# An attention and mixture-of-experts layer on one core: stores of q moved ahead of K's transfers, and each tile's rows turned between the halves of the tile before

## The chip, the cores and the metric

The kernel runs on one core of a Trainium2 chip. Its engines are TensorE (PE in the profile, its weight loads PEld), VectorE (DVE), ScalarE (ACT), GpSimd (POOL) and SyncE (SP), which here only issues transfers. The metric is the device time of one launch in microseconds (us), lower is better.

## The reference, cut to what matters

```python
# x (16,112,256); ctx (16,375,192); 16 heads of 16; 8 experts, 256 -> 512 -> 256, top 2
q = (layernorm(x) @ Wq);  k = ctx @ Wk;  v = ctx @ Wv          # per head
x = x + tanh(g_xattn) * (softmax(q k^T * hd**-0.5) v) @ Wo
xf = layernorm(x).reshape(b * s, d)                            # 1792 rows
probs = softmax(xf @ router_w.T);  keep the top 2, divide by their sum
h = silu(xf @ gate_w[e] + gate_b[e]) * (xf @ up_w[e] + up_b[e])
y = sum over the two chosen e of probs[e] * (h @ down_w[e] + down_b[e])
x = x + tanh(g_ffn) * y
```

## The kernel before, in words

**Precision.** Nearly every factor is split into a high part and a rest (`kH`/`kL`, `xH`/`xL`, `GH`/`GL`, `DH`/`DL`, `hH`/`hL`). A product is three matmuls: high by high, high by rest, rest by high. ACT makes the high part, DVE then subtracts it from the source for the rest.

**Attention.** First q is made for all 16 batches in four groups of four; `store_q(g)` writes group g to the DRAM scratch `q_scr` in four transfers, from where the heads are read back in another layout. Then a software pipeline runs in steps (`step`, one batch enters per step). In step n the context of batch n+2 is loaded (`load_ctx`), q of batch n is read (`queries`, six transfers and one for the bias row), K of batch n goes from `kH` and `kL` into `KS` (`keys`, eight transfers and four, which wait for ACT's and DVE's parts), and the negated row maxima of batch n-1 go into `QS` (line 306). All these transfers are issued by SP, strictly in the order of the code. The groups 2 and 3 of q are stored in steps 2 and 3, and step 4 (`FIRST - 1`) begins with a wait for them (line 288). From step 4 on, one expert's gate and up weights are loaded (line 291, `wsq`) in two steps of three; ACT squares and sums them (line 479, slot 4 of a step), for a scale per expert. ACT also takes the exponentials (line 496) on which PE's transposed scores (line 633) wait.

**Experts.** The rows are sorted by expert into 21 tiles of 256 rows (at most one expert a tile); POOL gathers a tile's rows (`xt`) and adds its results back (`acc_scr`). A step s handles three tiles: tile s is turned (four transposes, line 1347) and split into `xH` (ACT, line 1276) and `xL` (DVE, line 1506), and two small DVE operations pick its row weights; tile s-1 gets its gate and up matmuls (line 1363, 48 of them in two halves, `q` = 0 and 1, with a bank pair each), ACT's `sg` (line 1286, four chunks, a half makes two), DVE's `hf` (line 1523), then `hH` (ACT, line 1293) and `hL` (DVE, line 1529); tile s-2 gets its down matmuls (line 1376, 24), and `ys` on DVE (line 1538) and twice on ACT (line 1301). ACT and DVE work strictly in the order of their code.

**Arriving weights.** The first 8 steps are written out, and in them tile t < 8 needs expert t at most. While they run, the weights of expert s+1 are split in step s: `high(n)` on ACT (line 1033) and `low(n)` on DVE (line 1045) for gate (n even) and up (n odd), `down_high` and `down_low` (lines 1038 and 1052) for the down weights. Three raw buffers (`WB`) hold gate and up weights, so SP's load n waits for `low(n-3)`. PE's gate and up matmuls of tile t wait for `xL` of tile t, for `low(2t+1)`, and, for each half, for that half's `hf` of tile t-1:

```python
                        pe.wait_ge(v_x, t + 1)
                        if isinstance(i, int) and t < E:
                            pe.wait_ge(e_l, 2 * (t + 1))
                        for q in range(FQ):
                            wait(pe, a_s, FC * (t - 1) + FB * (q + 1))
                            wait(pe, v_h, FC * (t - 1) + FB * (q + 1))
```

Steps 8 to 19 are a loop on the engines, and 20 to 22 are written out again. At a step's start each of PE, DVE and ACT reads the tile's expert number from memory into a register (line 1159).

## Time and profile before

| | |
|---|---|
| median of 3 runs | 592.64 us (591.18 to 600.44) |
| the profiled execution, its own time | 591.52 us |
| its span, first to last instruction | 589.8 us |
| busy share of the span: PE, DVE, ACT, POOL | 83%, 72%, 58%, 50% |
| attention, with the first normalisation | 0 to about 340 us |
| routing | about 340 to 369 us |
| experts' tiles; copy to the output | 369 to about 575 us; the rest |

The profiled execution took 591.52 us, of which its instructions span 589.8; the 1.7 us around them are the launch. A stage's time is read from when its instructions start and end in the time-ordered list, and what an engine waited for stands in brackets at the end of its row.

### The profile page before, as it was taken

The numbers are of one execution on the slowest core, as the hardware profiler recorded it, in microseconds if no ns is written. First come the engines' busy times: TensorE is split into PE (matmuls) and PEld (weight loads), VectorE is DVE, ScalarE is ACT, GpSimd is POOL, SyncE is SP. The second block draws the span as 40 slices with busy tenths as digits, with TensorE's granted clock in tenths as the row PEclk, the third lists the DMA queues.
The fourth block names the chain that finished last, engine by engine and source line by source line (L and its number), as shares of the span: only waits on it lengthen the run. The fifth ranks groups of instructions, "written<-read, shape, count | busy, mean of one in ns | idle before, by whom it ended". The sixth has DMA issues, their size and how long they took to land. (4 is left out here: it accounts for less than half of the span.)

```text
span 589.8 us, 15126 instructions
## 1 busy us (share of the span) xinstructions
PE 487.2 (83%) x4723; PEld 437.1 (74%) x4724; DVE 427.2 (72%) x902; ACT 340.1 (58%) x638; POOL 293.0 (50%) x252
## 2 busy tenths in 40 slices
PE   4888897999999999999989721697899999999930
PEld 3767886888888888888868621596799999999920
DVE  4865897899998989989997678678775555555520
ACT  5743565766677666767654590767575545545410
POOL 5182555454565544564544323606457565555440
PEclk9997999999999999999995855799899999999985
DMA  8764668664566456446323086846524443343234
GB/s 205 184 151 104 167 163 181 175 165 112 136 139 180 92 162 177 114 102 159 74 48 103 23 303 192 297 161 168 155 37 75 72 62 54 62 71 54 28 37 133
DMA packets 69022, 74.88 MB, mean 127 GB/s; under 512 B 28744, under 2 KB 57248, under 8 KB 68784
## 3 DMA queue, kind: packets, MB, share of 16 engines
q1 hardware_dynamic: 60912, 63.23, 40.4%
q0 software_dynamic: 8064, 11.06, 11.3%
q8 instruction: 27, 0.44, 0.3%
q14 instruction: 19, 0.16, 0.1%
HBM read 42.51 MB, written 14.98 MB: 97 GB/s over the span
## 5 line engine op out<-in xcount | busy, mean ns | idle before, releaser
L363 POOL TENSOR_TENSOR PL<-PT 125x448 f16<-125x448 f32 x96 | 100.6, 1051 | 135.7 <-ACT PT L496 135.7
L496 ACT ACTIVATE PT<-bank 125x448 f32<-125x448 f32 x192 | 103.9, 544 | 85.1 <-PE bank L633 84.3
L790 DVE TENSOR_REDUCE mx<-bank 112x1 f32<-112x375 f32 x256 | 130.8, 542 | 24.6 <-PE bank L615 22.8
L1244 POOL DMA_INDIRECT acc_scr<-ys,slot_row x42 | 69.1, 1645 | 84.0 <-ACT ys L1301 75.1
L615 PE MATMUL bank<-KS,QS 97*112 97x376 f32 x256 | 91.5, 377 | 12.9 <-DVE mx L790 11.7
L633 PE MATMUL bank<-QS,KS 98*125 98x256 f32 x384 | 84.3, 304 | 4.7 <-ACT PT L496 3.1
L1363 PE MATMUL bank<-xH,GH 128*128 128x256 f16 x336 | 65.4, 277 | 7.7 <-ACT sg L1286 5.9
L633 PEld LDWEIGHTS bank<-QS,KS 98*125 98x125 f32 x384 | 67.0, 194 | 6.3 <-ACT PT L496 3.8
L1363 PE MATMUL bank<-xH,GL 128*128 128x256 f16 x336 | 65.3, 277 | 0.0
L1363 PE MATMUL bank<-xL,GH 128*128 128x256 f16 x336 | 65.2, 277 | 0.0
L615 PEld LDWEIGHTS bank<-KS,QS 97*112 97x112 f32 x256 | 45.5, 182 | 26.0 <-DVE mx L790 23.5
L780 DVE TENSOR_TENSOR PL<-PT 125x448 f16<-125x448 f32 x96 | 57.8, 618 | 6.5 <-ACT PT L496 6.4
L1058 POOL DMA_INDIRECT xt<-xn_scr,slot_row x42 | 45.8, 1091 | 30.8 <-DVE slot_row L1476 18.3
L652 PE MATMUL bank<-VS,PT 125*128 125x49 bf16 x768 | 52.1, 188 | 2.8 <-DVE PL L780 2.1
L1286 ACT ACTIVATE sg<-bank,gb,inv 128x256 f32<-128x256 f32 x84 | 42.5, 560 | 19.6 <-PE bank L1363 18.2
L1523 DVE SCALAR_TENSOR_TENSOR hf<-bank,ub,sg 128x256 f32<-128x256 f32 x84 | 37.5, 480 | 19.1 <-ACT sg L1286 18.2
L652 PE MATMUL bank<-VS,PL 125*128 125x49 bf16 x768 | 50.5, 185 | 0.0
L652 PEld LDWEIGHTS bank<-VS,PT 125*128 125x128 bf16 x768 | 39.4, 100 | 13.3 <-DVE PL L780 2.4
L1363 PEld LDWEIGHTS bank<-xH,GH 128*128 x336 | 33.3, 99 | 13.4 <-issue 9.1
L1301 ACT ACTIVATE ys<-ys,slot_weight 128x256 f32<-128x256 f32 x42 | 19.0, 500 | 41.9 <-DVE ys L1538 41.9
L1529 DVE TENSOR_TENSOR hL<-hf,hH 128x1024 fp32r<-128x1024 f32 x21 | 25.8, 1227 | 23.6 <-ACT hH L1293 23.6
L652 PEld LDWEIGHTS bank<-VS,PL 125*128 125x128 f16 x768 | 38.2, 97 | 0.0
(215 smaller groups left out, 1076.0 us busy)
## 6 DMA issues: line engine op xcount, KB each, us to landing
KS<-kH SPq DMA_DIRECT2D x128, 94.0 KB, 2.2
KS<-kL SPq DMA_DIRECT2D x64, 94.0 KB, 2.2
QS<-q_scr SPq DMA_DIRECT2D x96, 56.0 KB
ctx_sb<-in_ctx SPq DMA_DIRECT2D x16, 281.2 KB
wsq<-in_L_ffn_gate_w SPq DMA_DIRECT2D x8, 512.0 KB, 3.7
wsq<-in_L_ffn_up_w SPq DMA_DIRECT2D x8, 512.0 KB, 4.9
w_raw<-in_L_ffn_gate_w SPq DMA_DIRECT2D x8, 512.0 KB, 6.1
w_raw<-in_L_ffn_up_w SPq DMA_DIRECT2D x8, 512.0 KB, 4.3
```

The lines of the kernel that those rows point to most:

```text
L363: pool.tensor_tensor(PL[:, 2 * k:2 * k + 2, :, 0:N], PT[:, 2 * k:2 * k + 2, :, 0:N], PH[:, 2 * k:2 * k + 2, :, 0:N], ALU.subtract).then_in ...
L496: act.activation(PT[:, 2 * k:2 * k + 2, :, 0:N].rearrange("p a e i -> p (a e) i"), psST[k % 2][0:JP].rearrange("p (a i) -> p a i", i=NI)[: ...
L615: pe.matmul(psS[hd % 2][0:N, 0:MP], QS[u][0:RM, hd // 2, hd % 2, 0:N], KS[u][0:RM, hd // 2, :], start=True, stop=True).then_inc(p_S, 1)
L633: mm = pe.matmul(psST[k % 2][0:JP, 2 * NI * a:2 * NI * (a + 1)], KS[u][0:RM + 1, p, JP * t:JP * (t + 1)], QS[u][0:RM + 1, p, :, :].rearran ...
L652: mm = pe.matmul(psO[hd // 8][:, VW * (hd % 8):VW * (hd % 8 + 1)], P[:, JT * p + t, e, :], VS[:, u, t, hd, :], start=(part == 0 and t == 0 ...
L780: dve.tensor_tensor(PL[:, 2 * k:2 * k + 2, :, 0:N].rearrange("p a e i -> p (a e) i"), PT[:, 2 * k:2 * k + 2, :, 0:N].rearrange("p a e i -> ...
L790: dve.tensor_reduce(mx[:, hd:hd + 1], psS[hd % 2][0:N, 0:M], AX.X, ALU.max).then_inc(v_max, 1)
L1058: pool.indirect_dma_start(xt[:, t % XR, k, :], None, xn_scr, bass.IndirectOffsetOnAxis(ap=slot[:, TH * t + k:TH * t + k + 1].bitcast(U32), ...
L1244: pool.indirect_dma_start(acc_scr, bass.IndirectOffsetOnAxis(ap=slot[:, TH * t + k:TH * t + k + 1].bitcast(U32), axis=0), ys[:, u, k, :], ...
L1286: act.activation(sg[:, f, :], bG[f // FB][:, TS * (f % FB):TS * (f % FB + 1)], ACT.Silu, bias=gb[:, bass.ds(e * FC + f, 1)], scale=inv[:, ...
L1363: mm = pe.matmul(bank[:, TS * (f % FB):TS * (f % FB + 1)], w.rearrange("p o f -> p (o f)"), x[:, u, k, :], start=(n == 0 and k == 0), stop ...
L1523: dve.scalar_tensor_tensor(out=hf[:, f, :], in0=bU[f // FB][:, TS * (f % FB):TS * (f % FB + 1)], scalar=ub[:, bass.ds(e1 * FC + f, 1)], in ...
```

## The change

It has two parts.

1. In steps 2 and 3 of the attention, `store_q` of groups 2 and 3 (batches 8 to 15) is issued after the step's `queries` and before its `keys`, where it was issued at the step's end.
2. In the experts' steps the turning of tile s, with its `xH` and `xL`, moves from ahead of the matmuls of tile s-1 to between their halves (new functions `turn`, `rows_high`, `rows_low`); on ACT and DVE it stands after the first two chunks. The weight splits move too: `high(2s+2)` follows `xH`, `down_high` follows the fourth chunk, `high(2s+3)` goes behind `hH`; on DVE `low(2s+1)`, which belonged to the step before, now follows `xL` of tile s, `down_low` follows the fourth chunk and `low(2s+2)` stands behind `hL`. Step 0 has no tile in its halves: there the rows stand as before, then `high(2)`, `down_high(1)` and `high(3)`, and on DVE `down_low(1)` and `low(2)`. No operation is added or removed.

```diff
@@ -299,14 +299,14 @@
                     if live(i, c, 0):
                         if not starts(i, c):
                             queries(i, c)
+                            if isinstance(i, int) and 1 < NB * i + c < GROUPS:
+                                store_q(NB * i + c)
                             keys(i, c)
                     if live(i, c, 1):
                         b, h, u = at(i, c - 1)
                         sp.wait_ge(v_nm, b + 1)
                         sp.dma_start(f32(QS[u][RM:RM + 1, :, :, 0:N]).rearrange("o q e i -> o (q e) i"),
                                      f32(nm[:])).then_inc(d_m[u], 16)
-                    if isinstance(i, int) and 1 < NB * i + c < GROUPS:
-                        store_q(NB * i + c)
...
@@ -1150,6 +1150,10 @@
             return isinstance(i, int) and UN * i + c + 1 < E
+        def arrived(i, c):
+
+            return isinstance(i, int) and 0 < UN * i + c < E
...
@@ -1264,20 +1268,20 @@
...
+                def rows_high(i, c):
+                    t, h, u = at(i, c)
+                    act.wait_ge(k_T, t + 1)
+                    wait(act, k_GU, FQ * (t - 1))
+                    act.activation(xH[:, u], bT[u][:, 0:DC * TS].rearrange("p (c s) -> p c s", c=DC), ACT.Copy,
+                                   scale=XS).then_inc(a_x, 1)
+
                 def step(i, c):
...
-                    if has(i, c, 0):
-                        t, h, u = at(i, c)
-                        act.wait_ge(k_T, t + 1)
-                        wait(act, k_GU, FQ * (t - 1))
...
-                    if arriving(i, c):
-                        high(act, 2 * (UN * i + c + 1))
-                        high(act, 2 * (UN * i + c + 1) + 1)
+                    if has(i, c, 0) and not has(i, c, 1):
+                        rows_high(i, c)
                     if has(i, c, 1):
                         t, h, u = at(i, c - 1)
                         for f in range(FC):
@@ -1286,13 +1290,21 @@
...
                                            ).then_inc(a_s, 1)
-                            if f == FB - 1 and arriving(i, c):
-                                down_high(act, UN * i + c + 1)
+                            if f == FB - 1:
+                                if has(i, c, 0):
+                                    rows_high(i, c)
+                                if arriving(i, c):
+                                    high(act, 2 * (UN * i + c + 1))
+                        if arriving(i, c):
+                            down_high(act, UN * i + c + 1)
                         act.wait_ge(v_h, FC * (t + 1))
                         wait(act, k_D, t - 1)
                         act.activation(hH[:, u], hf[:], ACT.Copy).then_inc(a_h, 1)
                     elif arriving(i, c):
+                        high(act, 2 * (UN * i + c + 1))
                         down_high(act, UN * i + c + 1)
+                    if arriving(i, c):
+                        high(act, 2 * (UN * i + c + 1) + 1)
                     if has(i, c, 2):
...
@@ -1333,20 +1345,23 @@
...
+                def turn(i, c):
+                    t, h, u = at(i, c)
+                    x4, h4 = c % XR, i + c // XR
+                    pe.wait_ge(l_x[x4], 16 * TH * (h4 + 1))
+                    wait(pe, v_x, t - 1)
+                    for s in range(TH):
+                        for k in range(DC):
+                            mm = pe.transpose(bT[u][:, TS * k + 128 * s:TS * k + 128 * (s + 1)],
+                                              xt[:, x4, s, 128 * k:128 * (k + 1)], ident[:])
+                    mm.then_inc(k_T, 1)
+
                 def step(i, c):
                     if isinstance(i, int) and UN * i + c == 1:
                         pe.wait_ge(e_te, 1)
                     e1, e2 = two_experts(pe, i, c, kept)
-                    if has(i, c, 0):
-                        t, h, u = at(i, c)
...
-                        mm.then_inc(k_T, 1)
+                    if has(i, c, 0) and not has(i, c, 1):
+                        turn(i, c)
                     if has(i, c, 1):
                         t, h, u = at(i, c - 1)
                         pe.wait_ge(v_x, t + 1)
@@ -1364,6 +1379,8 @@
...
                             mm.then_inc(k_GU, 1)
+                            if q == 0 and has(i, c, 0):
+                                turn(i, c)
                     if has(i, c, 2):
...
@@ -1495,26 +1512,26 @@
...
+                def rows_low(i, c):
+                    t, h, u = at(i, c)
+                    x4, h4 = c % XR, i + c // XR
+                    dve.wait_ge(a_x, t + 1)
+                    dve.scalar_tensor_tensor(out=xL[:, u], in0=bT[u][:, 0:DC * TS].rearrange("p (c s) -> p c s", c=DC),
+                                             scalar=XS, in1=xH[:, u], op0=ALU.mult, op1=ALU.subtract
+                                             ).then_inc(v_x, 1)
+                    dve.wait_ge(l_x[x4], 16 * TH * (h4 + 1))
+                    wait(dve, a_y, TH * (t - UN + 1))
+                    dve.tensor_tensor(both_w[:, c % UN], xt[:, x4, :, DIM:ROWW],
+                                      which[:, bass.ds(TH * t, TH), :], ALU.mult).then_inc(v_b, 1)
+                    dve.wait_ge(v_b, t + 1)
+                    dve.tensor_reduce(wt[:, c % UN, :], both_w[:, c % UN], AX.X, ALU.add).then_inc(v_w, 1)
+
...
                 def step(i, c):
                     e1, e2 = two_experts(dve, i, c, kept)
-                    if has(i, c, 0):
-                        t, h, u = at(i, c)
...
-                        dve.tensor_reduce(wt[:, c % UN, :], both_w[:, c % UN], AX.X, ALU.add).then_inc(v_w, 1)
-                    if arriving(i, c):
-                        low(dve, 2 * (UN * i + c + 1))
-                        low(dve, 2 * (UN * i + c + 1) + 1)
+                    if has(i, c, 0) and not has(i, c, 1):
+                        rows_low(i, c)
                     if has(i, c, 1):
                         t, h, u = at(i, c - 1)
                         wait(dve, v_l, t)
@@ -1523,12 +1540,19 @@
...
                                                      op0=ALU.add, op1=ALU.mult).then_inc(v_h, 1)
-                            if f == FB - 1 and arriving(i, c):
-                                down_low(dve, UN * i + c + 1)
+                            if f == FB - 1:
+                                if has(i, c, 0):
+                                    rows_low(i, c)
+                                if arrived(i, c):
+                                    low(dve, 2 * (UN * i + c) + 1)
+                        if arriving(i, c):
+                            down_low(dve, UN * i + c + 1)
                         dve.wait_ge(a_h, t + 1)
                         dve.tensor_tensor(hL[:, u], hf[:], f32(hH[:, u]), ALU.subtract).then_inc(v_l, 1)
                     elif arriving(i, c):
                         down_low(dve, UN * i + c + 1)
+                    if arriving(i, c):
+                        low(dve, 2 * (UN * i + c + 1))
                     if has(i, c, 2):
```

In the blocks below, a row is an instruction or a run of equal ones in the engine's own order.

SP in the attention, from step 2's context load to step 4's first weight load, before (QS2, KS2 are batch 2's buffers, QS0, KS0 batch 3's):

```order
L260 DMA QS2<-q_scr 16x8x112 x6
L264 DMA KS2<-bias_scr 1x8x376
L278 DMA KS2<-kH 32x2x376 x8
L278 DMA KS2<-kL 32x2x376 x4
L306 DMA QS1<-nm 1x16x112
L329 DMA q_scr<-qP 128x4x112 x4
L252 DMA ctx_sb<-in_ctx_768 125x576
L260 DMA QS0<-q_scr 16x8x112 x6
```

and now:

```order
L260 DMA QS2<-q_scr 16x8x112 x6
L264 DMA KS2<-bias_scr 1x8x376
L329 DMA q_scr<-qP 128x4x112 x4
L278 DMA KS2<-kH 32x2x376 x8
L278 DMA KS2<-kL 32x2x376 x4
L308 DMA QS1<-nm 1x16x112
L252 DMA ctx_sb<-in_ctx_768 125x576
L260 DMA QS0<-q_scr 16x8x112 x6
```

The four stores moved ahead of K's twelve transfers; step 3 changes alike, so that the last thing ahead of step 4's wait is the transfer of `nm`.

DVE in step 2 of the experts (tile 2 turned, tile 1 in its halves), before:

```order
L1506 SCALAR_TENSOR_TENSOR xL<-bank,xH 128x512
L1511 TENSOR_TENSOR both_w<-xt,slot_choice 128x4
L1514 TENSOR_REDUCE slot_weight<-both_w 128x2
L1045 SCALAR_TENSOR_TENSOR GL<-w_raw,sc,GH 128x1024 x2
L1523 ISA
L1523 SCALAR_TENSOR_TENSOR hf<-bank,ub,sg 128x256
```

and now:

```order
L1540 SCALAR_TENSOR_TENSOR hf<-bank,ub,sg 128x256
L1519 SCALAR_TENSOR_TENSOR xL<-bank,xH 128x512
L1524 TENSOR_TENSOR both_w<-xt,slot_choice 128x4
L1527 TENSOR_REDUCE slot_weight<-both_w 128x2
L1045 SCALAR_TENSOR_TENSOR GL<-w_raw,sc,GH 128x1024
L1540 ISA
```

The first row now is the second chunk of `hf`: two chunks come ahead of `xL`, and one `GL` follows instead of two. The other stands at the step's end, between `hL` and the finished tile's `ys`:

```order
L1052 TENSOR_TENSOR DL<-DL,DH 128x1024
L1551 TENSOR_TENSOR hL<-hf,hH 128x1024
L1045 SCALAR_TENSOR_TENSOR GL<-w_raw,sc,GH 128x1024
L1562 ISA
L1562 SCALAR_TENSOR_TENSOR ys<-misc,inv,dbB 128x512
L1163 TENSOR_LOAD tile_e
```

The order on DVE is so: two chunks, rows, one rest, two chunks, `DL`, `hL`, one rest, `ys`; and ACT goes into the next step's `sg` right after its `ys`.

PE at the start of a step and in its first half, before:

```order
L1159 TENSOR_LOAD tile_e
L1159 ISA x2
L1347 MATMUL bank0<-ident,xt 128x128 x4
L1363 ISA
L1363 MATMUL bank2<-xH,GH 128x256
```

and now:

```order
L1163 TENSOR_LOAD tile_e
L1163 ISA x2
L1378 ISA
L1378 MATMUL bank2<-xH,GH 128x256
L1378 ISA
```

and, now, between the halves:

```order
L1378 MATMUL bank4<-xH,GL 128x256
L1355 MATMUL bank0<-ident,xt 128x128 x4
L1378 ISA
L1378 MATMUL bank3<-xH,GH 128x256
L1378 ISA
```

The transposes no longer stand between the read of the expert number and the first matmul that uses it.

## Rows read from the trace of the kernel before

**Rows 1.** Busy time by stretch, steps 4 and 5 of the attention: stretch, length, then each engine's busy us, granted clock, DMA share, GB/s.

```profile
82.10:102.80 20.70, 16.01 (x182) 14.16 (x183) 16.34 (x35) 12.12 (x22) 9.24 (x9) 1.00 0.76 180
102.80:120.70 17.90, 16.67 (x188) 14.93 (x188) 16.32 (x36) 12.74 (x25) 9.30 (x9) 1.00 0.68 173
```

**Rows 2.** SP in order of time, steps 2 to 4: start, length, then what it issued.

```profile
53.02 0.70 SPq L264 DMA_DIRECT2D KS<-bias_scr  x1
57.72 6.10 SPq L278 DMA_DIRECT2D KS<-kH  x8
...
74.49 5.18 SPq L278 DMA_DIRECT2D KS<-kH  x8
...
83.34 2.74 SPq L329 DMA_DIRECT2D q_scr<-qP  x4
88.73 0.38 SPq L291 DMA_DIRECT2D wsq<-in_L_ffn_gate_w  x1
```

**Rows 3.** ACT and PE in order of time, step 4 of the attention.

```profile
95.59 1.91 ACT L479 ACTIVATE wsq<-wsq 128x2048 f32<-128x2048 f32 x1 [2.93 <-DMA wsq<-in_L_ffn_up_w]
...
98.07 0.50 PE L633 MATMUL bank<-QS,KS 98*125 98x256 f32 x2 [2.48 <-ACT PT L496]
```

**Rows 4.** The chain that ended last: gate and up matmuls of tiles 2, 3, 7, 8.

```profile
391.33 5.44 PE bank L1363 x48
...
402.02 5.44 PE bank L1363 x48
...
442.82 5.24 PE bank L1363 x48
...
451.35 5.24 PE bank L1363 x48
```

**Rows 5.** Start of the tiles, in order of time, on DVE, PE and ACT.

```profile
370.78 0.69 DVE L1506 SCALAR_TENSOR_TENSOR xL<-bank,xH 128x512 f16<-128x512 f32 x1 [3.63 <-ACT xH L1276]
...
373.13 1.11 PE L1347 MATMUL bank<-ident,xt 128*128 128x128 f32 x4 [3.01 <-DMA xt<-xn_scr,slot_row]
...
376.60 0.40 PE L1363 MATMUL bank<-xH,GH 128*128 128x256 f16 x2
...
379.39 1.28 ACT L1286 ACT_TABLE_LOAD   x1
```

**Rows 6.** ACT in order of time, from the end of step 4 of the tiles.

```profile
406.74 0.91 ACT L1301 ACTIVATE ys<-ys,slot_weight 128x256 f32<-128x256 f32 x2 [1.95 <-DVE ys L1538]
407.55 0.57 ACT L1276 ACTIVATE xH<-bank 128x512 f16<-128x512 f32 x1
...
410.11 1.00 ACT L1286 ACTIVATE sg<-bank,gb,inv 128x256 f32<-128x256 f32 x2
```

**Rows 7.** DVE in order of time, step 5 of the tiles.

```profile
408.16 0.69 DVE L1506 SCALAR_TENSOR_TENSOR xL<-bank,xH 128x512 f16<-128x512 f32 x1 [1.46 <-ACT xH L1276]
...
409.20 2.48 DVE L1045 SCALAR_TENSOR_TENSOR GL<-w_raw,sc,GH 128x1024 f16<-128x1024 f32 x2
411.60 0.87 DVE L1523 SCALAR_TENSOR_TENSOR hf<-bank,ub,sg 128x256 f32<-128x256 f32 x2
412.39 1.22 DVE L1052 TENSOR_TENSOR DL<-DL,DH 128x1024 fp32r<-128x1024 f32 x1
...
415.51 1.23 DVE L1529 TENSOR_TENSOR hL<-hf,hH 128x1024 fp32r<-128x1024 f32 x1 [1.12 <-ACT hH L1293]
416.65 0.75 DVE L1538 SCALAR_TENSOR_TENSOR ys<-misc,inv,dbB 128x512 f32<-128x512 f32 x1
```

**Rows 8.** A weight load at the loop's turn; the last tile's first matmul; line 1159's register reads, min/median/max ns.

```profile
476.52 0.42 PEld L1347 LDWEIGHTS bank<-ident,xt 128*128 128x128 f32 x4 [0.26 <-issue]
...
553.50 0.39 PE L1363 MATMUL bank<-xH,GH 128*128 128x256 f16 x2
...
L1159 PEldq TENSOR_LOAD <-tile_e x25: 297/306/488, 369.0 to 551.4; - x25
```

**Rows 9.** All transfers of raw gate and up weights, `w_raw`, from issue to landing.

```profile
DMA to landing us min/median/max: 3.6/5.0/7.4
```

More of the change, by code:

```diff
@@ L1271, in step @@
                         e = expert(act, UN * i + c - 1)
-                    if has(i, c, 0):
-                        t, h, u = at(i, c)
-                        act.wait_ge(k_T, t + 1)
-                        wait(act, k_GU, FQ * (t - 1))
-                        act.activation(xH[:, u], bT[u][:, 0:DC * TS].rearrange("p (c s) -> p c s", c=DC), ACT.Copy,
-                                       scale=XS).then_inc(a_x, 1)
-                    if arriving(i, c):
-                        high(act, 2 * (UN * i + c + 1))
-                        high(act, 2 * (UN * i + c + 1) + 1)
+                    if has(i, c, 0) and not has(i, c, 1):
+                        rows_high(i, c)
                     if has(i, c, 1):
@@ L1339, in step @@
                     e1, e2 = two_experts(pe, i, c, kept)
-                    if has(i, c, 0):
-                        t, h, u = at(i, c)
-                        x4, h4 = c % XR, i + c // XR
-                        pe.wait_ge(l_x[x4], 16 * TH * (h4 + 1))
-                        wait(pe, v_x, t - 1)
-                        for s in range(TH):
-                            for k in range(DC):
-                                mm = pe.transpose(bT[u][:, TS * k + 128 * s:TS * k + 128 * (s + 1)],
-                                                  xt[:, x4, s, 128 * k:128 * (k + 1)], ident[:])
-                        mm.then_inc(k_T, 1)
+                    if has(i, c, 0) and not has(i, c, 1):
+                        turn(i, c)
                     if has(i, c, 1):
@@ L1501, in step @@
                     e1, e2 = two_experts(dve, i, c, kept)
-                    if has(i, c, 0):
-                        t, h, u = at(i, c)
-                        x4, h4 = c % XR, i + c // XR
-                        dve.wait_ge(a_x, t + 1)
-                        dve.scalar_tensor_tensor(out=xL[:, u], in0=bT[u][:, 0:DC * TS].rearrange("p (c s) -> p c s", c=DC),
-                                                 scalar=XS, in1=xH[:, u], op0=ALU.mult, op1=ALU.subtract
-                                                 ).then_inc(v_x, 1)
-                        dve.wait_ge(l_x[x4], 16 * TH * (h4 + 1))
-                        wait(dve, a_y, TH * (t - UN + 1))
-                        dve.tensor_tensor(both_w[:, c % UN], xt[:, x4, :, DIM:ROWW],
-                                          which[:, bass.ds(TH * t, TH), :], ALU.mult).then_inc(v_b, 1)
-                        dve.wait_ge(v_b, t + 1)
-                        dve.tensor_reduce(wt[:, c % UN, :], both_w[:, c % UN], AX.X, ALU.add).then_inc(v_w, 1)
-                    if arriving(i, c):
-                        low(dve, 2 * (UN * i + c + 1))
-                        low(dve, 2 * (UN * i + c + 1) + 1)
+                    if has(i, c, 0) and not has(i, c, 1):
+                        rows_low(i, c)
                     if has(i, c, 1):
```

## The prediction

> **What bounds the kernel now.** I read the time-ordered lists of each engine beside the chain that ended last, stage by stage, since the stages have different limits. In the attention PE sets the pace, and a step with a square on ACT takes 17.90 us; step 4 takes 20.70 [rows 1]. The reader is to see why: ACT stood 2.93 us ahead of its square, until the up weights had landed, and PE stood 2.48 us for the exponential that ACT has behind it [rows 3]. The weights were late because SP issued them at 88.73, after it had waited for the stores of q's last group, which it had issued at 83.34 [rows 2]. In the experts' stage the chain shows three rhythms. From tile 8 on PE is full: 8.53 us from one tile's gate and up matmuls to the next, 442.82 to 451.35 [rows 4]. From tile 2 to tile 3 it is 10.69, and from tile 3 (402.02) to tile 7 (442.82) 40.80 for four tiles [rows 4]: there PE waits for `hf` of the tile before, which DVE reaches only behind two weight rests. And the stage starts slowly: the first gate and up matmuls stand behind the turning of tile 1, whose rows arrived at 373.13 [rows 5], though tile 0 was ready.
>
> **The stores of q.** Nothing is added; four transfers move past K's twelve and past `nm` in steps 2 and 3. The store takes SP 2.74 us to issue [rows 2]. In step 2 it falls into a hole: SP was done with the bias row at 53.72 and stood until 57.72 for `kH` [rows 2], 4.0 us against 2.74, so K starts no later. In step 3 one store leaves the queue ahead of the loads and one enters behind them, so K's start at 74.49 [rows 2] moves by nothing or by a few tenths. Then step 4's wait finds the stores, issued by about 74.5, long landed. The weights go out right behind `nm`, at about 83.4 instead of 88.73, 5.3 us earlier [rows 2]; they were 2.93 us late for ACT [rows 3], which leaves 2.4 us in hand. What is late next is nothing that steps 5 and following do not have too, so step 4 falls to the length of step 5: 20.70 - 17.90 = **2.8 us** [rows 1]. Bounds: 2.93, ACT's whole wait, and 0, if K's transfers of step 3 come so late that PE waits for them in step 4 instead. Here I take 2.8, as it is the difference of two whole steps.
>
> **The start of the tiles.** `xL` of tile 0 is done at 370.78 + 0.69 = 371.5 [rows 5]. A handover from DVE to PE I put at 0.2, an estimate, so the first half starts at 371.7; before, it stood behind the transposes at 373.13, 1.11 us long, and began near 374.0 [rows 5]. A half is 24 matmuls, 5.24 / 2 = 2.6 us at the full clock [rows 4] and twice that, 5.2, at the half clock, which the rows show until 376.60, when pairs fall to 0.40 [rows 5]. If the clock rises no later than then, the half ends at 376.8; if it rises earlier by the 2.3 us that PE starts earlier (374.3), at 375.8. I take 376.2. Then follows what had been hidden in part: ACT's table load, 1.28 us [rows 5], which stands behind the wait for PE's half. After it come two `sg` 0.90 to the next start and `xH` 0.57 [rows 6], `xL` with the two small operations 0.95 (1.04 lie between the starts of `xL` and `GL`, part of it a wait), one rest 1.28 (half of 2.40 and the last 0.08) [rows 7], and 0.3 for the handovers from PE and to PE: 1.28 + 0.90 + 0.57 + 0.95 + 1.28 + 0.3 = 5.3. So tile 1's matmuls start at 376.2 + 5.3 = 381.5. From there PE is full for two tiles: 381.5 + 2 x 8.53 = 398.6 for tile 3, where the chain has 402.02 [rows 4]. That is **3.4 us**; bounds 2.8 and 3.8 from the clock's two cases.
>
> **The lap of the arriving weights.** From tile 3 on a lap runs through DVE and ACT. It begins with the first `hf`. Two chunks 0.87 [rows 7], during which ACT does the second `sg` and `xH`, so `xL` starts 0.91 after the lap did. `xL` and the small operations take 0.9 to 1.04, one rest 1.20, two chunks 0.8, `DL` 1.14, `hL` 1.14, the other rest 1.20, `ys` 0.75 [rows 7]; these are lengths less the 0.08 by which rows that follow each other overlap (411.60 + 0.87 against 412.39). `hH` lies beside `DL` and costs nothing: before, DVE stood 1.12 for it ahead of `hL` [rows 7]; now `DL` (1.14) covers just that. Then ACT's two `ys` 0.82 and the first `sg` 0.56 [rows 6] lead back to `hf`. Sum: 0.91 + 0.95 + 1.20 + 0.80 + 1.14 + 1.14 + 1.20 + 0.75 + 0.82 + 0.56 = 9.5 us. PE needs 8.53, so the lap still sets the pace, and PE's wait moves from `hf` to `low(2t+1)`. Four tiles take 38.0 instead of 40.80 [rows 4]: **2.8 us**. The raw weights keep up: each load is issued a lap less one rest before its use, about 7 us or more, and such transfers landed in 5.0 in the median and 7.4 at most [rows 9].
>
> **The turned tile between the halves.** From tile 8 on the edit removes nothing, since PE is full. It must not add either. The read of the expert number (0.306 us [rows 8]) had 0.44 us of transposes behind it, and now stands right ahead of matmuls that need it. The trace has one place like that: the last tile has nothing to turn, and its first matmul starts at 553.50 with no idle time in its row [rows 8]. At the loop's turn, with two reads and a branch, PE stood 0.26 even with the transposes [rows 8]; there I add 0.1 for each of two turns, **0.2 us**. The bounds are 0 and 0.26 + 0.31 for each of 13 tiles, 7.4 us, and I stay by the last tile's row, which shows the case itself. The Trainium skill ("DMA: Bandwidth & Descriptors", section "Latency and other measured facts") puts the floor of such a register read at some 600 ns; by it, exposed at 13 tiles, 7.8 us would be lost and the time would be about 591, an estimate. The row shows 306 ns and hides it.
>
> **Sum.** 591.52 - 2.8 - 3.4 - 2.8 + 0.2 = 582.7 for an execution like the profiled one. That one lay 1.1 us under the median of 592.64; with half of that back I forecast **583.3**, 1.6% less.
>
> **The rivals.** (1) *One of the 2.8 us terms does not come.* Either the lap stays at 10.7, because a large weight transfer lands late or ACT's `sg` after its `ys` waits for its register, or step 4 keeps its length, because the early weights land late beside q's and K's loads. For it speaks that both hang on landings that spread from 3.6 to 7.4 us [rows 9]; against it the margins of 2.4 us and of some 2 us above. Each gives 583.3 + 2.8 = 586.1. (2) *PE never waits.* If the chunks overlap more than the rows show, tiles 3 to 7 cost 34.1 instead of 38.0: 579.4. Against it: DVE's own work in the lap is 8.1 us by the sum above, and ACT's 1.4 behind it are exposed by the order of the code. (3) *PE's sequencer loses its lead,* and the kernel ends slower. The place is the step's start and the turn between the halves, both now with waits and address work close to dependent matmuls. The price is the read, 0.31, and a hole like the one at the loop's turn, 0.26, on either side of the turned tile [rows 8]: 0.83 for each of 13 tiles, 10.8 us, so 594.1. It decides from 9.3 / 13 = 0.72 us a tile. Against it stands the last tile's row, and that before the change PE's 48 matmuls went through in one piece [rows 4]. (4) *The change does not do what it says:* if the stall in step 4 was not the stores' doing, the wait of 2.93 stays; that is in (1).
>
> **How the numbers follow.** Chances: the forecast, 581.0 to 586.0, 0.60; rival 1, 586.1 and up to 588 with a bad start, 0.20; rival 2, 0.09; rival 3, 0.04; anything else, to either side, 0.07. The range 579.0 to 589.0 takes in the first three. A measurement of this kernel tells about 2% from no change, that is under 580.8 or over 604.5. Faster by over 2%: rival 2 and the forecast's lower tail, 0.13; slower by over 2%: 0.02, from the rest alone; within 2%: 0.85.
>
> **What would show it.** Right: ACT's square in step 4 with no wait for the weights, and the step 17.9 long; the first gate and up matmul near 371.7 less 2.8, and tile 1's some 9.8 later; four laps of about 9.5 with `GL` as what releases PE's matmuls; 8.53 from tile 8 on. Wrong: K's transfers as what releases the scores in step 4, laps over 10, idle time of PE named "issue" at each tile, or a first half that runs at the half clock for long.

## The result, and the profile after

The changed kernel takes 587.85 us in the median, 0.9884 of the kernel before (95% interval 0.9838 to 0.9930); a second series of it, on another occasion, gave 0.9885 (0.9833 to 0.9936). By that it is 1.16% faster, 6.9 us on the 592.64 shown above, where 9.3 us (1.6%) were forecast. Its profiled execution took 587.68 us with a span of 585.9, against 591.52 and 589.8. These two executions differ by only 3.9 us of span: by stages the attention's steps are 3.4 shorter, the routing 2.2 and the tiles 4.05, but what lies ahead of the first transpose of maxima took 4.25 more (52.81 against 48.56) and what follows PE's last matmul of the tiles 1.5 more, and in neither does the change alter an operation.

**Attention.** The windows of steps 4 and 5 [rows 1], from one step's first transpose of its maxima to the next's:

```profile
86.83:104.52 17.69, 15.78 (x182) 14.18 (x183) 16.13 (x35) 12.11 (x22) 9.29 (x9) 1.00 0.63 159
104.52:122.38 17.86, 16.64 (x187) 14.88 (x188) 16.30 (x36) 12.75 (x25) 9.27 (x9) 1.00 0.65 172
```

Step 4 is as short as step 5; the same two windows were 20.70 and 17.90. SP's list [rows 2] shows both stores ahead of `kH`, and the gate weights issued right behind `nm`:

```profile
58.51 2.18 SPq L329 DMA_DIRECT2D q_scr<-qP  x4
62.49 5.92 SPq L278 DMA_DIRECT2D KS<-kH  x8
...
76.28 2.21 SPq L329 DMA_DIRECT2D q_scr<-qP  x4
79.27 5.17 SPq L278 DMA_DIRECT2D KS<-kH  x8
...
87.51 0.56 SPq L308 DMA_DIRECT2D QS<-nm  x1
88.20 0.50 SPq L291 DMA_DIRECT2D wsq<-in_L_ffn_gate_w  x1
```

ACT's square of that step [rows 3] has no bracket any more, so it waited for nothing:

```profile
97.32 1.92 ACT L479 ACTIVATE wsq<-wsq 128x2048 f32<-128x2048 f32 x1
```

**Start of the tiles** [rows 5], in order of time. Tile 0's first gate and up matmuls come 2.62 us behind its turn (367.64), where it was 5.04.

```profile
370.26 0.60 PE L1378 MATMUL bank<-xH,GH 128*128 128x256 f16 x2 [1.50 <-DVE xL L1519]
...
375.23 0.60 PE L1355 MATMUL bank<-ident,xt 128*128 128x128 f32 x4
375.52 1.28 ACT L1290 ACT_TABLE_LOAD   x1 [3.11 <-PE bank L1378]
...
379.26 1.27 DVE L1045 SCALAR_TENSOR_TENSOR GL<-w_raw,sc,GH 128x1024 f16<-128x1024 f32 x1
...
380.73 0.41 PE L1378 MATMUL bank<-xH,GH 128*128 128x256 f16 x2 [2.29 <-DVE GL L1045]
...
381.63 0.38 PE L1378 MATMUL bank<-xL,GH 128*128 128x256 f16 x2
381.85 0.56 PE L1378 MATMUL bank<-xH,GL 128*128 128x256 f16 x2
382.20 0.63 PE L1378 MATMUL bank<-xH,GH 128*128 128x256 f16 x2
```

At 380.73 PE has stood 2.29 us for tile 1's `GL`. It starts in pairs of 0.38, and then at 381.85 the pairs become 0.56 and 0.63: the clock has gone from its upper level (2.4 GHz) to the lower (1.2 GHz). The forecast had these matmuls at full speed. In the kernel before, the clock stayed up at tile 1, behind a shorter wait:

```profile
382.60 0.40 PE L1363 MATMUL bank<-xH,GH 128*128 128x256 f16 x2 [1.46 <-DVE hf L1523]
```

**The tiles** [rows 4], in the chain. A tile now has two pieces of 24 matmuls; the first of tiles 0, 1, 2, 3, 7 and 8:

```profile
370.26 5.14 PE bank L1378 x24
...
380.73 4.24 PE bank L1378 x24
...
391.14 2.63 PE bank L1378 x24
...
399.69 2.64 PE bank L1378 x24
...
436.79 2.64 PE bank L1378 x24
...
445.33 2.64 PE bank L1378 x24
```

Counted from the turn of tile 0, tile 3 stands at 32.05 (33.02 before), tile 7 at 69.15 (73.82), tile 8 at 77.69 (82.35). So 1.0 us came from the start and 3.7 from the lap. Not all of it lasts: in the old order the count to a tile holds the transposes of the next one too. At the end that evens out: tile 20's transposes, which stood ahead of tile 19, now stand between its halves, so tile 20 follows it after 8.54 us instead of 8.09. From the turn of tile 0 to PE's last matmul of the tiles it is 193.39 against 197.44, 4.05 less. DVE's lap [rows 7], from one tile's first `hf` to the next's:

```profile
405.80 0.88 DVE L1540 SCALAR_TENSOR_TENSOR hf<-bank,ub,sg 128x256 f32<-128x256 f32 x2 [1.61 <-ACT sg L1290]
406.60 0.68 DVE L1519 SCALAR_TENSOR_TENSOR xL<-bank,xH 128x512 f16<-128x512 f32 x1
...
407.45 1.28 DVE L1045 SCALAR_TENSOR_TENSOR GL<-w_raw,sc,GH 128x1024 f16<-128x1024 f32 x1
408.65 0.87 DVE L1540 SCALAR_TENSOR_TENSOR hf<-bank,ub,sg 128x256 f32<-128x256 f32 x2
409.46 1.22 DVE L1052 TENSOR_TENSOR DL<-DL,DH 128x1024 fp32r<-128x1024 f32 x1
410.64 1.25 DVE L1551 TENSOR_TENSOR hL<-hf,hH 128x1024 fp32r<-128x1024 f32 x1
411.82 1.27 DVE L1045 SCALAR_TENSOR_TENSOR GL<-w_raw,sc,GH 128x1024 f16<-128x1024 f32 x1
413.01 0.74 DVE L1562 SCALAR_TENSOR_TENSOR ys<-misc,inv,dbB 128x512 f32<-128x512 f32 x1
415.36 0.88 DVE L1540 SCALAR_TENSOR_TENSOR hf<-bank,ub,sg 128x256 f32<-128x256 f32 x2 [1.61 <-ACT sg L1290]
```

It is 9.56 long, and DVE rests in it only for the last 1.61: ACT's two `ys` and first `sg`. From tile 8 to 19 the kernel takes 94.43 us (94.23 before).

### The profile page after: what moved, and what is told of

Read it like the earlier page. It is cut to its first block and busy times, and to the rows that moved or that the text cites. A ratio compares the mean times of both kernels' runs of the same rounds, so it can differ in the third digit from the quotient of the medians.

```text
span 585.9 us, 15126 instructions
## 1 busy us (share of the span) xinstructions
PE 487.2 (83%) x4723; PEld 436.4 (74%) x4724; DVE 427.8 (73%) x902; ACT 340.6 (58%) x638; POOL 290.4 (50%) x252
## 5 line engine op out<-in xcount | busy, mean ns | idle before, releaser
L1248 POOL DMA_INDIRECT acc_scr<-ys,slot_row x42 | 67.0, 1595 | 82.6 <-ACT ys L1313 73.6
L615 PE MATMUL bank<-KS,QS 97*112 97x376 f32 x256 | 91.7, 380 | 12.5 <-DVE mx L790 11.5
L633 PE MATMUL bank<-QS,KS 98*125 98x256 f32 x384 | 82.9, 300 | 2.0 <-DMA QS<-nm 0.9
```

The source lines that it names most:

```text
L615: pe.matmul(psS[hd % 2][0:N, 0:MP], QS[u][0:RM, hd // 2, hd % 2, 0:N], KS[u][0:RM, hd // 2, :], start=True, stop=True).then_inc(p_S, 1)
L633: mm = pe.matmul(psST[k % 2][0:JP, 2 * NI * a:2 * NI * (a + 1)], KS[u][0:RM + 1, p, JP * t:JP * (t + 1)], QS[u][0:RM + 1, p, :, :].rearran ...
L1248: pool.indirect_dma_start(acc_scr, bass.IndirectOffsetOnAxis(ap=slot[:, TH * t + k:TH * t + k + 1].bitcast(U32), axis=0), ys[:, u, k, :], ...
```

## Experiments

Each was timed against the kernel before. The table reads the time-ordered list of each profile (0.15 us under the chain's figures at tile 8): when the gate and up matmuls of tiles 1 and 8 begin, in us behind the turn of tile 0; how long PE stood ahead of tile 1; and the distance from tile 1 to 2.

| kernel | ratio to before (95%) | tile 1 | idle | 1 to 2 | tile 8 |
|---|---|---|---|---|---|
| before | 1 | 13.60 | 1.46 | 8.73 | 82.18 |
| changed | 0.9884 (0.9838 to 0.9930) | 13.09 | 2.29 | 10.25 | 77.54 |
| after_again | 0.9885 (0.9833 to 0.9936) | 12.91 | 2.28 | 10.24 | 77.36 |
| stores_only | 0.9925 (0.9883 to 0.9967) | 13.50 | 0.27 | 8.82 | 82.08 |
| experts_only | 0.9956 (0.9903 to 1.001) | 14.50 | 4.11 | 11.29 | 79.99 |
| rows_only | 0.9968 (0.9931 to 1.0006) | 13.12 | 2.66 | 10.25 | 82.89 |
| pe_filled | 0.9892 (0.9837 to 0.9948) | 14.49 | 1.53 | 8.55 | 77.26 |
| pe_filled_ahead | 0.9840 (0.9780 to 0.9901) | 10.32 | 2.29 | 10.22 | 74.76 |
| pe_filled_all | 0.9766 (0.9709 to 0.9822) | 10.41 | 0.41 | 8.55 | 73.17 |
| silu_early | 0.9882 (0.9820 to 0.9944) | 12.38 | 2.00 | 10.21 | 76.81 |
| ys_later | 0.9815 (0.9763 to 0.9866) | 12.89 | 2.29 | 10.25 | 74.38 |
| silu_ys | 0.9763 (0.9692 to 0.9834) | 11.91 | 1.03 | 8.58 | 71.77 |
| best | 0.9723 (0.9658 to 0.9788) | 9.08 | 0 | 8.54 | 68.86 |
| read_twice | 0.9909 (0.9862 to 0.9957) | 13.26 | 2.29 | 10.23 | 78.31 |

### The two parts alone

stores_only is the kernel before with these lines of the change and no others (what stands between them is left out):

```diff
                             queries(i, c)
+                            if isinstance(i, int) and 1 < NB * i + c < GROUPS:
+                                store_q(NB * i + c)
...
-                    if isinstance(i, int) and 1 < NB * i + c < GROUPS:
-                        store_q(NB * i + c)
```

> The kernel before with only the stores of q moved; the experts' stage is the old one. Theory: the store of q's last group was the whole stall of step 4, and nothing else hangs on it. ACT's square in step 4 then waits for nothing, the attention from the first to the last maximum transpose (267.5 us in the profile of before, 264.2 after) takes 264.2 to 264.7, the tiles keep their old rhythm (10.7 and 40.8 for four), and the kernel is 2.8 us shorter than before, a ratio of 0.995. Rival: the stores moved ahead of K's loads hold these up in steps 2 and 3, and part of the gain in step 4 is given back there: attention 266 or more, ratio 0.998 to 1.000.

Its windows of steps 4 and 5:

```profile
82.13:99.81 17.68, 15.77 (x182) 14.18 (x183) 16.12 (x35) 12.11 (x22) 9.28 (x9) 1.00 0.65 158
99.81:117.71 17.90, 16.68 (x188) 14.92 (x188) 16.29 (x36) 12.76 (x25) 9.28 (x9) 1.00 0.65 172
```

Step 4 is down to 17.68. The attention took 264.37 us from first to last of these transposes (267.58 before), and the tiles kept their old rhythm. The theory holds; nothing was given back in steps 2 and 3 (16.83 and 16.79 long, before 16.73 and 16.77). The ratio's interval takes in the expected 0.995.

experts_only is the changed kernel with those lines put back.

> The changed kernel with the stores of q back in their old place. Theory: the experts' part alone is worth 4.7 us, as in the profile after, from the turn of tile 0 to the matmuls of tile 8 (82.35 before, 77.69 after), because the clock falls again in tile 1. Ratio 0.992, and together with the stores alone the two ratios multiply to that of the whole change, 0.988. Rival A: the fall of the clock in tile 1 was chance of that one execution; then the stretch takes 76.0 and the ratio is 0.990 or below. Rival B: the two parts are not independent (earlier ends of the attention are eaten in the routing), and the two ratios multiply to less than 0.985 or more than 0.991.

The ratios multiply to 0.9881, as the whole change has 0.9884, so nothing speaks for rival B, though the intervals are too wide to rule it out. This profile has a lower granted clock in parts of the attention (0.901 in the mean of the span, 0.925 in that of the changed kernel), so only its tiles are read. PE at tile 1:

```profile
392.98 0.60 PE L1378 MATMUL bank<-xH,GH 128*128 128x256 f16 x2 [4.11 <-DVE GL L1045]
```

The clock is low in tile 1 here too, behind the longest idle time of the table, against rival A. But the theory's stretch was missed: 79.99, not 77.7, so the tiles gained 2.2 us and not 4.7. ACT took up its table 2.1 us behind the end of PE's first half, where it was 0.3 in the changed kernel, and the hole grew by that; the code of the tiles is the same.

after_again is the changed kernel itself.

> The changed kernel once more, as it is, for a second profile and a tighter ratio. In four profiles with the new experts' stage, the stretch from tile 2's gate and up matmuls on repeats to 0.02 us, but tile 1's matmuls started 12.4 to 14.5 us behind the turn of tile 0. Theory: what lies ahead of tile 2 varies from run to run by some 2 us (ACT's first Silu begins 0.3 to 2.1 us behind the end of PE's first half), and the stage before the tiles takes either 50.3 or 52.8 us; the rest repeats: attention 264.2, four tiles 37.1. The stretch from the turn of tile 0 to tile 8's matmuls is again between 76.5 and 80. Rival: a given kernel always has the same start, and the differences among the kernels are due to their edits; then this profile shows 13.09 and 77.69 again.

The rival holds for the start: 12.91, 2.28, 10.24 and 77.36 repeat the first profile to 0.2 us. Two profiles of one kernel can't exclude that the start varies, and experts_only, with the same code there, had another. The stages around it do vary, with code that is the same: up to the first transpose of maxima 48.21 to 52.81 us over all profiles, and from the last one to the turn of tile 0 50.17 to 56.79. So the time of one execution can't be compared to a microsecond; its tiles can, from tile 2 on, where the same code repeats to 0.15 us.

### Tile 1 and the clock

pe_filled adds, behind tile 0's second half, matmuls into a free part of PSUM:

```diff
+                def fill(n):
+                    for k in range(n):
+                        pe.matmul(bY[1][:, 0:256], GH[:, 0, 0, 0, 0:128], GH[:, 0, 0, 0, 0:256],
+                                  start=True, stop=True)
...
+                        if isinstance(i, int) and t == 0:
+                            fill(20)
```

> The changed kernel with 20 more matmuls of the shape of the gate and up ones, behind tile 0's second half, into a part of PSUM that nobody reads; they add work and no result. PE stood 2.29 us there in the profile after; 20 of these are 2.2 us at the full clock (5.24 us for 48). Theory: the idle time is what lets the clock fall in tile 1. With PE busy, tile 1's first half runs at pairs of 0.38 us all through and takes 2.6 us instead of the 4.0 from 380.73 to 384.76, tile 2's matmuls start 8.6 to 8.8 us behind tile 1's instead of 10.41, and the whole is 1.6 us shorter than the changed kernel: turn of tile 0 to tile 8's matmuls 76.1. Rival: the clock falls at that moment whatever PE does just before (the fall came 6.2 us behind its rise at 375.6): the slow stretch is again in tile 1's first half, and the stretch stays at 77.7, or is longer if the added matmuls hold up tile 1's.

PE's list behind tile 0:

```profile
380.38 2.35 PE L1348 MATMUL misc<-GH 128*128 128x256 f16 x20
384.26 0.41 PE L1383 MATMUL bank<-xH,GH 128*128 128x256 f16 x2 [1.53 <-issue]
```

Tile 1's matmuls begin at 384.26 and tile 2's 8.55 later: with the hole cut to 1.53 the clock stays up, and the theory's mechanism holds. The rival, a fixed moment whatever PE does, falls: by the granted clock in windows of 0.1 us, the changed kernel's fall came 6.8 us behind the rise in tile 0, and at that distance the clock stayed up here, in silu_ys and in the kernel before. The theory's time, 76.1, doesn't show (77.26), since tile 1 itself began 1.4 us later (14.49): ACT took up the table at 379.05, though PE's first half had ended by the turn at 377.33. In the changed kernel the two are 375.52 and 375.23. In the profiles with the new order where ACT waits at this place the gap is 0.3 us in eight and 1.3, 1.7 and 2.1 in silu_early, pe_filled and experts_only; what ACT waits for there is open.

pe_filled_ahead leaves those out and fills ahead of tile 0 instead, with `fill(40)` in front of the turn of tile 0 and `fill(11)` behind it; pe_filled_all does both, with 18 behind tile 0.

> The changed kernel with added matmuls that nobody reads (shape of the gate and up ones, into a free part of PSUM) wherever PE stands at the start of the tiles: 40 between the routing's last matmuls and the turn of tile 0 (7.25 us of idle time), 11 behind the turn of tile 0 (1.50 us), 18 behind tile 0's second half. They add work and no result. Theory: the half clock of tile 0's first half is the price of PE's idle time ahead of it. With PE busy the clock rises before the turn of tile 0; the turn takes 0.6 instead of 1.1, tile 0's first half 2.6 instead of 5.0 to 5.1, tile 1's matmuls start 10.1 to 10.6 us behind the turn of tile 0 instead of 13.09, tile 2's 8.6 to 8.8 behind them, and the stretch to tile 8 is 73 instead of 77.69. Ratio 0.980. Rival: ACT and DVE, with the raw weights' landing, set tile 1's start anyway, and it stays at 12.4 or later: 76. Second rival: the clock rises at a moment that added work does not move, and tile 0's first half takes 5 again.

> As the kernel with PE filled everywhere, but without the 18 matmuls behind tile 0's second half: only the 40 ahead of the turn of tile 0 and the 11 behind it stay. It tells whether an idle time of about 2.5 us lets the clock fall again when PE has been at the full clock for long before. Theory: it is the idle time, whatever went before, so tile 1's first half, which starts at 10.41 behind the turn, falls to the half clock again shortly after its start, as at 381.85 in the profile after; tile 2's matmuls start 10.2 behind tile 1's and the stretch to tile 8 is 74.9. Rival: the clock fell in tile 1 because PE had been at the full clock for only some 3 us when it stood; with 10 us of work behind it, it holds: 8.55 and 73.2.

PE in pe_filled_all, then in pe_filled_ahead at tile 1:

```profile
362.66 6.50 PE L1348 MATMUL misc<-GH 128*128 128x256 f16 x40
370.14 0.66 PE L1360 MATMUL bank<-ident,xt 128*128 128x128 f32 x4 [0.97 <-DMA xt<-xn_scr,slot_row]
370.64 1.36 PE L1348 MATMUL misc<-GH 128*128 128x256 f16 x11
372.31 0.41 PE L1385 MATMUL bank<-xH,GH 128*128 128x256 f16 x2 [0.30 <-DVE xL L1530]
...
374.95 0.60 PE L1360 MATMUL bank<-ident,xt 128*128 128x128 f32 x4
```

```profile
379.11 0.40 PE L1385 MATMUL bank<-xH,GH 128*128 128x256 f16 x2 [2.29 <-DVE GL L1045]
...
379.84 0.64 PE L1385 MATMUL bank<-xH,GH 128*128 128x256 f16 x2
```

Filled, the turn takes 0.66 instead of 1.11 and tile 0's first half 2.64 (372.31 to 374.95) instead of 4.97: half clock at the start was the price of standing ahead of it, 2.7 us at tile 1. With some 15 us of nearly unbroken work behind it PE still fell to the half clock after 2.29 us of standing, at 0.7 us into tile 1; the theory holds, its rival doesn't. Both kernels land on their expected stretch (73.17 for 73, 74.76 for 74.9). The Trainium skill ("TensorE: Matmul & The Clock Gate", section "Part 1: The HAM clock gate (the "warmup" mystery)") says that the clock follows how busy PE has lately been, and puts the loss while it rises at under 1% of a typical kernel. The first the runs bear out. The second they don't contradict: the fills took 4.2 to 4.4 us out of the stretch to tile 8, 0.7% of 588; by the ratios it is 1.2% (0.9766 against 0.9885), with about 0.6% to either side of each.

silu_early lets ACT take up its table while it has nothing to do (`warm` is a new tile of one column that nobody reads):

```diff
                 down_high(act, 0)
+                act.activation(warm[:], sc[:, 0:1], ACT.Silu)
```

> The changed kernel with one more activation on ACT, a Silu of one column into an unused tile, behind the first high part of the down weights and ahead of the rows of tile 0, while ACT has nothing else to do. It adds work and no result. In the profile after, ACT took up the table only once PE's first half was done: 1.28 us at 375.52, all of it exposed, since sg, xH, xL and GL follow one from the other up to tile 1's matmuls. Theory: the table load moves in front of the wait, tile 1's matmuls start 1.2 to 1.3 us earlier behind the turn of tile 0 (13.09 in the profile after, now 11.8), PE stands 1.0 instead of 2.29, and if the clock hangs on that idle time, it may stay up: the stretch to tile 8 is then 1.3 to 2.9 us shorter than 77.69. Rival: DVE's rest GL of the up weights waits for something else (the raw weights' landing), and tile 1's matmuls start as before; or ACT goes back to another table for its copies and the load stands again at 375.5.

PE's list at tile 1:

```profile
378.85 0.41 PE L1380 MATMUL bank<-xH,GH 128*128 128x256 f16 x2 [2.00 <-DVE GL L1045]
...
379.74 0.51 PE L1380 MATMUL bank<-xL,GH 128*128 128x256 f16 x2
```

No table load stands in the tiles any more, but `sg` began 1.3 us behind the end of PE's first half (374.93, 373.62), the same unexplained gap, so tile 1 came only 0.7 us earlier and not 1.28. After 2.00 us of standing the clock fell again. The ratio doesn't tell it from the changed kernel.

### The lap

ys_later takes ACT's two `ys` with their waits, here put into a function `weigh`, out of it, in steps 2 to 6:

```diff
...
                                 if has(i, c, 0):
                                     rows_high(i, c)
+                                if isinstance(i, int) and 3 <= UN * i + c < E:
+                                    weigh(i, c - 1)
...
-                    if has(i, c, 2):
+                    if has(i, c, 2) and not (isinstance(i, int) and UN * i + c < E - 1):
+                        weigh(i, c)
```

> The changed kernel with ACT's two ys of a tile (0.82 us) taken out of the lap of the arriving weights: in steps 2 to 6 they move from the end of the step behind the first two sg and xH of the next step. Nothing is added. Theory, that of the prediction: the lap of 9.55 us closes through DVE's ys, ACT's two ys, ACT's first sg and DVE's hf. Without ACT's ys it is 8.7, hardly more than PE's 8.53; PE's waits of 0.7 to 0.9 at tiles 4 to 6 vanish, four tiles from 3 to 7 take 34.2 to 34.9 instead of 37.1, and the kernel is 2.3 to 2.9 us shorter than the changed one. Rival: the lap is DVE's own work (8.1 by the sum of its rows) with the handovers, and takes 9.3 or more whatever ACT does; then four tiles stay at 37.

PE's first halves of tiles 3, 4 and 5 in its chain:

```profile
402.16 2.64 PE bank L1383 x24
...
410.70 2.64 PE bank L1383 x24
...
419.24 2.64 PE bank L1383 x24
```

From tile 2 to tile 8 every tile takes 8.54, and PE is never late: from tile 3 to 8 42.70 us, where the changed kernel has 45.65. The ratio falls by 0.007, less than the intervals can tell, but the trace has it. So the lap closed through ACT's `ys`, as the prediction had it.

rows_only keeps the turned tile between the halves, but puts the high and low parts of the arriving weights back where they were (shown for DVE; ACT's high parts go back alike):

```diff
+                    if arriving(i, c):
+                        low(dve, 2 * (UN * i + c + 1))
+                        low(dve, 2 * (UN * i + c + 1) + 1)
                     if has(i, c, 1):
...
-                                if arrived(i, c):
-                                    low(dve, 2 * (UN * i + c) + 1)
-                        if arriving(i, c):
-                            down_low(dve, UN * i + c + 1)
+                                if arriving(i, c):
+                                    down_low(dve, UN * i + c + 1)
...
-                    if arriving(i, c):
-                        low(dve, 2 * (UN * i + c + 1))
```

> The changed kernel with the turned tile between the halves, as changed, but the high and low parts of the arriving weights in their old order (two high and two low at the head of a step, the down weights' behind the second sg and hf). Theory: the gain in the lap comes from the order of the weights' low parts, not from the turn's place: DVE reaches hf only behind two low parts, and the lap stays at 10.2 to 10.7, 40.8 for four tiles, as before the change; only the start of the tiles is earlier, by 2.4 us. The kernel is then 3.7 us longer than the changed one, ratio to before 0.994. Rival: it is the turn's place that shortens the lap (PE and ACT are free of the next tile's rows at the head), and four tiles take 38 or less.

DVE's list in step 5:

```profile
420.11 2.49 DVE L1045 SCALAR_TENSOR_TENSOR GL<-w_raw,sc,GH 128x1024 f16<-128x1024 f32 x2 [2.02 <-ACT GH L1033]
422.51 0.87 DVE L1541 SCALAR_TENSOR_TENSOR hf<-bank,ub,sg 128x256 f32<-128x256 f32 x2
```

The lap is 11.08, longer than the old 10.70 and than the 10.2 to 10.7 of the theory: DVE stands 2.02 for both high parts, then does both low ones ahead of `hf`. The order of the weights' parts is the whole gain of the lap; the turn's new place alone loses 0.4 a lap.

### The register read

read_twice adds `expert(pe, UN * i + c - 1)` ahead of PE's reads in each step.

> The changed kernel with the expert's number read twice on PE at the head of each step, straight and in the loop; the second read's value alone is used. One more read (0.306 us in the median on PE's queue) with its register work and range test, about 0.5 us for each of 21 tiles. Theory, that of the prediction: PE's sequencer runs ahead of the matmuls far enough that one read more is hidden, except at the loop's turns: from tile 8's to tile 19's matmuls 94.4 to 94.9, where it was 94.43, and the time that of the changed kernel within 0.5 us. Rival: the lead is used up, and each read stands in front of its tile's first matmuls: 0.3 to 0.5 for each of 20 tiles, 100 to 104 from tile 8 to 19... that is 3.4 to 5.5 more in these eleven tiles (97.8 to 99.9), and 6 to 10 us on the whole.

PE's list, at tile 7 and tile 11:

```profile
439.26 0.41 PE L1380 MATMUL bank<-xH,GH 128*128 128x256 f16 x2 [0.43 <-issue]
...
474.47 0.41 PE L1380 MATMUL bank<-xH,GH 128*128 128x256 f16 x2 [0.88 <-issue]
```

Tiles 8 to 19 take 96.35, between the two expectations. Inside the loop's body and in the straight steps the tiles stay at 8.54, so a second read is hidden. Where the loop is entered, turns and is left (tiles 7, 11, 15 and 19) it costs 0.58, 0.81, 0.76 and 0.34. So the lead of PE's sequencer hides one read more in running code, and not where it branches. The Trainium skill ("DMA: Bandwidth & Descriptors", section "Latency and other measured facts") has a floor of some 600 ns for such a read; the 46 on PE's queue measured 0.304 in the median and 0.572 at most, and the measurement decides.

### Together

silu_ys has the early Silu and the moved `ys`; best has the three fills (40, 11, 11) as well.

> The changed kernel with the early Silu on ACT and ACT's ys moved, without added matmuls on PE. Theory: 77.5 less 0.6 (the early Silu, as measured alone) less 3.0 (the moved ys) gives 73.9 from the turn of tile 0 to tile 8's matmuls, with the half clock for tile 0's first half and again in tile 1; ratio 0.981. Rival: the clock's fall in tile 1 hangs on a moment that the earlier start shifts, and the stretch is 72.3 because tile 1's first half runs at the full clock.

silu_ys, PE's list at tile 1 and at the turn behind its first half:

```profile
380.25 0.43 PE L1385 MATMUL bank<-xH,GH 128*128 128x256 f16 x2 [1.03 <-issue]
...
382.92 0.60 PE L1362 MATMUL bank<-ident,xt 128*128 128x128 f32 x4
```

The rival's time came: the idle time ahead of tile 1 is 1.03, the clock held (first half 2.67), and the stretch is 71.77 where 72.3 was expected by the rival and 73.9 by the theory. Its reason, a moment that shifts, isn't shown, since the hole shrank as well. Part of this is luck: up to tile 1 the code is that of silu_early, where the hole was 2.00 and the clock fell, and the difference is ACT's gap behind PE's first half, 0.3 us here and 1.3 there. So the same start can come out on either side.

> The changed kernel with the three edits that gained alone, together: PE kept busy ahead of and in the start of the tiles by matmuls that nobody reads (40, 11 and here 11), one Silu of a column early on ACT, and ACT's ys of steps 2 to 6 behind the next step's first two sg. The added matmuls and the one Silu are work without a result; the reference's result is computed in full. Theory: the three act in different places and add up. From the turn of tile 0: tile 0's matmuls at 2.2, tile 1's at 9.1 (10.41 less the table load of 1.28), then PE full, 7 x 8.54 to tile 8: 69.0 against 77.4 to 77.7 of the changed kernel and 82.2 of the kernel before. The ratio to before is 0.9766 (filled) less 3.0 and 1.3 of 594, 0.969. Rival: with tiles 1 and 2 earlier, the raw weights land too late, since each load waits for the low part two before it; then PE stands at tiles 2 to 4 for the low parts and the stretch is 71 or more.

best, PE's list at the same place:

```profile
375.39 1.36 PE L1355 MATMUL misc<-GH 128*128 128x256 f16 x11
376.60 0.40 PE L1392 MATMUL bank<-xH,GH 128*128 128x256 f16 x2
...
379.23 0.60 PE L1367 MATMUL bank<-ident,xt 128*128 128x128 f32 x4
```

The three add up as expected: tile 1 at 9.08 (9.1), tile 8 at 68.86 (69.0), and the raw weights keep up. It computes the full result in 578.21 us, 2.8% under the kernel before and 1.6% under the changed one.

## Why the prediction was off

- **The stores of q, -2.8: right.** Step 4 became 3.0 us shorter, and the attention 3.4 (264.21 against 267.58); in the second profile and in stores_only it was 264.96 and 264.37, and 266.58 at most in the other profiles with the stores moved. SP's holes, the early weights and the square without a wait are as forecast.
- **The start of the tiles, -3.4: this step failed.** At tile 3 it brought 1.0. Tile 0 came 2.4 earlier, as forecast. Tile 1 stood at 13.09 behind the turn, where 381.5 was 12.5 (0.6 late). Then the prediction said "From there PE is full for two tiles: 381.5 + 2 x 8.53". PE is not full at the full clock there: by the chain, tile 1 to 2 took 10.41, 1.9 too much. Of the 0.6 before it, 0.5 is tile 0's first half, 4.97 us instead of 4.5: the clock rose 7.4 us behind the turn, near the later of the prediction's two cases (7.6 and 5.3). The sum had PE standing about 2 us between tile 0 and tile 1 and gave the clock no thought. That the standing is the cause is shown by pe_filled_all against pe_filled_ahead, which differ only in the 18 matmuls in that hole and start tile 1 within 0.1 us of each other: 8.55 and 10.22. With 1.03 of idle time it is 8.58. The edit itself made the hole. Before, PE came to tile 1 later and stood 1.46 us there, and the clock held; now tile 0 starts 2.4 us earlier and tile 1 only 0.5.
- **The lap, -2.8: the mechanism right, the size under.** Laps of 9.43 to 9.58 for 9.5 forecast, and `ys_later` shows that it closes where the prediction closed it. But only three of the four tiles counted have weights arriving ahead of them; the fourth took 8.56, and had taken 8.55 before, beside three of 10.7. So 37.10, not 38.0, and 3.7 saved. PE stands 0.73 to 0.88 a tile. The profile calls it "issue"; that it is `low(2t+1)` is read from its end, 408.73 ahead of tile 4 at 408.96.
- **Two loop turns, +0.2: right.** 94.43 against 94.23 from tile 8 to 19; rival 3 did not come.
- **Sum.** -3.4 (attention), -4.7 (tiles to 8) and +0.2 make -7.9 by the trace, where the forecast's terms make -8.8: the start 2.4 short, the lap 0.9 and the stores 0.6 over. The ratio says -6.9, with 2.7 us to either side. Of the 1.0 between them about 0.45 is what tile 20 gives back, which the prediction left out; the rest lies inside the interval.
- Of the rivals none came. The time itself, 587.85, lies in the band given to rival 1 (586.1 up to 588), but neither of the two terms that rival 1 doubts failed; that it lies there is luck. The prediction's own list of what would prove it wrong had "a first half that runs at the half clock for long"; it named the symptom and gave it no price.

## What to carry to other kernels

When an edit starts one piece of work earlier, work out how long the engine then stands before the next piece: here a PE hole of 2.0 to 2.7 us was paid twice, once as the hole and once as 1.7 us of half clock behind it, while holes of up to 1.5 us cost only themselves. That is no threshold: whether the hole's length alone decides, or also where it lies, no pair of runs separates. Find such holes at the start of a stage, and shorten them first by what feeds PE (a table taken up early, work of others moved out of the lap) and only then by idle matmuls. In a lap over two engines, look for the operation that nobody in the lap needs; here 0.8 us of ACT, moved aside, was worth 3 us over the arriving weights.

## What the runs showed of the hardware

- By the granted clock in windows of 0.1 us, PE's clock fell 0.6 to 1.3 us after the restart behind 2.00 to 2.29 us of idle time (six profiles, among them that of pe_filled_ahead, where PE had worked some 15 us before), 0.5 us after it behind 2.66 us (rows_only), and about 1.1 us before it, in the standing, behind 4.11 us (experts_only). It stayed up behind 0.27 (stores_only), 0.41, 1.03, 1.46 (before) and 1.53 us.
- ACT's table load stands behind the wait of the first Silu, and costs its full 1.28 us there, though ACT had stood 3.11 us. One Silu issued ahead takes it out of the tiles.
- ACT's first Silu or its table load began 0.3 us behind PE's first half in eight profiles and 1.3 to 2.1 in three; no row shows why. It stays open.
